# Edge convolutions of a graph network: maxima stored and edge attributes loaded in six pieces a turn

## The chip, the cores and the metric

The kernel runs on one core of one Trainium2 chip. The metric is the device time of one execution in microseconds (us), the median of several runs. TensorE (PE) does matrix products, VectorE (DVE) and ScalarE (ACT) work on vectors, GpSimd (POOL) here issues gathers by index, and SyncE (SP) issues plain transfers. All transfers share the core's 16 DMA engines.

## What is computed

A four-part graph network on 3125 nodes of 96 features and 50,000 edges, sorted by destination: 16 propagation steps, two layers of neighbour sums, a weighted neighbour sum, and at the end two edge convolutions, with a layer norm after each part. The change touches the edge convolutions alone:

```python
def _egnn_conv(x, src, dst, edge_attr, W_msg, W_edge, W_root, b):
    msg = x[src] @ W_msg + edge_attr @ W_edge
    agg = jax.ops.segment_max(msg, dst, num_segments=x.shape[0])
    agg = jnp.where(jnp.isneginf(agg), 0.0, agg)
    return agg + x @ W_root + b
c1 = jax.nn.leaky_relu(_egnn_conv(X, src, dst, edge_attr, W1_msg, W1_edge, W1_root, b1))
c2 = jax.nn.leaky_relu(_egnn_conv(c1, src, dst, edge_attr, W2_msg, W2_edge, W2_root, b2))
```

## The kernel before

The edges stand as 128 streams (one a partition) of T = 392 edges each. `edge_conv` runs once a layer. It goes over the 392 steps in TN = 14 turns of TURN = 28 tiles; a tile is 128 edges, one of each stream. Tiles 0 to 9 of a turn (PICKS = 10) get their source rows from PE: ten one-hot matrices times the table `yparts`, in 25 blocks of nodes (`pick`), and the edge term is added by `close`. Tiles 10 to 27 get theirs by 18 gathers that POOL issues from the table `y_table` in DRAM; their edge terms are made by PE in four groups of 5, 5, 5 and 3 tiles (`EGROUPS`, `edge_terms`), and DVE adds them (`add_terms`). DVE then runs the running maximum along the stream, tile by tile (`ran` counts the tiles). The one-hots of a turn are made by DVE (17 blocks) and ACT (8 blocks). At a turn's end ACT copies the picked rows out of PSUM (`take_rows`).

The work overlaps across turns: in turn k PE makes the edge terms of turn k and the picks of turn k + 1, POOL gathers for turn k + 1, each gather only after so many pick blocks are done (`used`), and DVE runs the maxima of turn k. The messages `msg` and the edge attributes `ea` have two buffers each, by the parity of the turn.

Three streams of transfers belong to a turn, all issued by SP in a fixed order:
- `store_run`: the running maxima go to DRAM (`run_max`), in two stores (`STORES`): tiles 0 to 19 (960 KB) when `ran` says that tile 20 is done, and tiles 20 to 27 (384 KB) at the turn's end.
- `load_ea`: the edge attributes of turn k + 2 come in one load of 896 KB, issued between the two stores, once PE has made the last edge terms of turn k (`terms`).

POOL and DVE write the buffer of turn k again in turn k + 2, after the semaphores `rst` of the stores; PE waits for `eal` of the load before `close` and `edge_terms`. At the layer's start SP issues both first loads and then the store of the node table to `y_table`, which POOL's first gather waits for (`yst`). At the layer's end POOL waits for all stores of `run_max` and then gathers 25 times from it (the last edge of each node), and the result is put together.

## Time and profile before

| | us |
|---|---|
| median of 3 runs | 2619.41 |
| lowest and highest | 2613.77, 2621.47 |
| the profiled execution | 2614.05 |
| its span | 2612.3 |
| edge convolution, layer 0 (1587.11 to 2096.30) | 509.2 |
| edge convolution, layer 1 (2096.30 to the end) | 516.0 |
| one turn (ACT's first copy to its first copy in the next turn) | 27.8 to 31.0 |
| mean granted clock of PE | 0.897 of full |

The profile is of one execution. Its time is the span and 1.75 us around it. Times of rows are us from the span's start. A row of the timeline gives start, duration, engine, line, operation, what it writes and reads, the number of merged instructions, and in brackets the engine's idle time before it and what ended that; "remote" stands for a semaphore whose sender the profile doesn't match, "issue" for idle time with no wait that it shows. "SPq" is a transfer's issue by SP. The ends of matmuls are modelled.

### The profile page before, as it was taken

The page shows a single profiled execution, that of the slowest core. Times are in us where ns is not written, and L with a number is a line of the kernel's source. Part 1 is how long each engine was busy: PE and PEld are TensorE (multiplying, and loading weights), DVE is VectorE, ACT ScalarE, POOL GpSimd, SP SyncE. Part 2 cuts the span into 40 slices and gives each one's busy share as a digit, 9 for nine tenths or more (in the row PEclk, how much of TensorE's full clock was granted, in tenths as well). Part 3 has the DMA queues.
Part 4 walks back from the last instruction along what each step waited for, and adds up shares of the span by engine and source line. Part 5 has one row for each costly group of instructions (what it writes and reads, how often), then busy time and mean ns, then how long its engine had stood idle before and what let it go on. Part 6 is the DMA issues. An engine that isn't in the chain of part 4 may idle for free. (4 is left out here: it accounts for less than half of the span.)

```text
span 2612.3 us, 54694 instructions
## 1 busy us (share of the span) xinstructions
PE 2108.3 (81%) x21375; PEld 1855.4 (71%) x21375; DVE 1616.7 (62%) x4651; ACT 879.5 (34%) x1209; POOL 1181.3 (45%) x997
## 2 busy tenths in 40 slices
PE   4494579999999999997876977888886578888860
PEld 4232279999999999997872436777776577777760
DVE  7999975555555555574572034766665356676656
ACT  0495510000000000001210005887784067788720
POOL 0200057887878777720000003666564346566641
PEclk9995579999999999998987986999998589999975
DMA  3592012323233223310007822344333034334321
GB/s 127 179 408 107 1 23 20 30 21 30 21 30 26 24 20 30 30 17 7 2 1 313 318 94 69 115 130 130 111 111 111 19 96 131 113 110 128 121 77 28
DMA packets 150904, 227.14 MB, mean 87 GB/s; under 512 B 87649, under 2 KB 109825, under 8 KB 147106
## 3 DMA queue, kind: packets, MB, share of 16 engines
q1 hardware_dynamic: 70994, 186.72, 19.6%
q0 software_dynamic: 74688, 28.51, 11.4%
q10 hardware_dynamic: 5008, 9.07, 1.1%
q8 instruction: 134, 2.20, 0.3%
q14 instruction: 80, 0.66, 0.1%
HBM read 123.37 MB, written 100.84 MB: 86 GB/s over the span
## 5 line engine op out<-in xcount | busy, mean ns | idle before, releaser
L615 PE MATMUL ps<-parts,at 128*128 128x192 f16 x11250 | 948.1, 248 | 23.4 <-POOL at L647 13.4
L615 PEld LDWEIGHTS ps<-parts,at 128*128 128x128 f16 x11250 | 940.3, 99 | 25.6 <-issue 24.0
L1622 PE MATMUL ps<-yparts,source_onehots_c 128*128 128x192 f16 x7000 | 675.5, 253 | 129.8 <-issue 110.0
L1413 POOL DMA_INDIRECT messages_c<-y_table,srci_sb x504 | 495.6, 983 | 571.9 <-DMA y_table<-ytab 259.4
L1622 PEld LDWEIGHTS ps<-yparts,source_onehots_c 128*128 128x128 f16 x7000 | 590.0, 101 | 199.6 <-issue 156.8
L656 POOL DMA_INDIRECT weight_matrix<-w,place x392 | 608.7, 1553 | 162.2 <-issue 95.6
L1441 ACT ACTIVATE source_gaps_c<-sources_spread,unshift 128x1280 f16<-128x1280 f16 x216 | 294.8, 1365 | 19.3 <-PE ps L1622 3.2
L739 DVE SCALAR_TENSOR_TENSOR t<-ps,coef,g 128x96 f32<-128x96 f32 x400 | 127.0, 317 | 250.3 <-PE ps L615 211.6
L1444 ACT ACTIVATE source_onehots_c<-source_gaps_c 128x1280 f16<-128x1280 f16 x216 | 274.4, 1270 | 6.9
L684 ACT ACTIVATE ea_limbs<-ea_in,ea_scale 128x392 f16<-128x392 f32 x32 | 19.9, 621 | 744.0 <-DMA ea_in<-in_eaT 738.8
L1496 DVE TENSOR_SCALAR source_onehots_c<-sources_spread,shift 128x1280 f16<-128x1280 f16 x484 | 264.9, 557 | 0.3
L1545 DVE SCALAR_TENSOR_TENSOR messages_c<-messages_c,brk 128x96 f32<-128x96 f32 x784 | 249.3, 318 | 18.2
L605 PE MATMUL ps<-onekey,oneplace 128*128 128x200 f16 x784 | 154.9, 359 | 80.5 <-DVE oneplace L560 80.5
L605 PEld LDWEIGHTS ps<-onekey,oneplace 128*128 128x128 f16 x784 | 78.9, 122 | 156.4 <-DVE oneplace L560 108.1
L1516 DVE TENSOR_TENSOR messages_c<-picked_pairs_c 128x192 f32<-128x192 f32 x140 | 49.2, 351 | 175.2 <-issue 132.3
L1244 PE MATMUL ps<-weights,x_sb 128*96 128x512 f32 (+1 forms) x350 | 137.1, 555 | 24.0 <-DMA weights<-weight_matrix 24.0
L742 DVE SCALAR_TENSOR_TENSOR t<-ps,coef,t 128x96 f32<-128x96 f32 x400 | 127.2, 318 | 14.1
L1524 DVE TENSOR_TENSOR messages_c<-messages_c,ps 128x480 f32<-128x480 f32 x112 | 67.1, 599 | 108.1 <-remote 102.6
L1244 PEld LDWEIGHTS ps<-weights,x_sb 128*96 128x96 f32 x350 | 55.2, 165 | 106.1 <-issue 81.8
L749 DVE CAST parts<-t 128x96 f16<-128x96 f32 x375 | 92.4, 246 | 55.6 <-DVE t L742 1.0
L1453 ACT ACTIVATE picked_pairs_c<-ps 128x384 f32<-128x384 f32 x140 | 57.7, 498 | 192.7 <-remote 153.5
L647 POOL TENSOR_TENSOR at<-at,ident 128x128 f16<-128x128 f16 x25 | 10.8, 470 | 244.5 <-issue 244.5
(359 smaller groups left out, 1540.2 us busy)
## 6 DMA issues: line engine op xcount, KB each, us to landing
weight_matrix<-blank SPq DMA_DIRECT2D x27, 1600.0 KB
weights<-weight_matrix SPq DMA_DIRECT2D x27, 1600.0 KB, 9.6
run_max<-messages_c SPq DMA_DIRECT2D x28, 960.0 KB
ea_c<-edge_limbs SPq DMA_DIRECT2D x28, 896.0 KB
edge_limbs<-ea_limbs SPq DMA_DIRECT2D x128, 98.0 KB
run_max<-messages_c SPq DMA_DIRECT2D x28, 384.0 KB
sources_spread<-sources_by_tile ACTq DMA_DIRECT2D x26, 320.0 KB
messages_c<-y_table,srci_sb POOLq DMA_INDIRECT x504
```

The source lines that it names most:

```text
L605: nc.tensor.matmul(m.ps[:, n % 8, 256 * (s % 2):256 * (s % 2) + KEYS], oneplace[:, q % RING, h, :, j], onekey[:, q % RING, h, :, j], start ...
L615: mm = nc.tensor.matmul(m.ps[:, bank, 0:2 * D], m.at[:, s, blk * P:(blk + 1) * P], parts[:, s, :], start=(s == 0), stop=(s == NB - 1))
L656: nc.gpsimd.indirect_dma_start(cells, bass.IndirectOffsetOnAxis(m.place[:, t:t + 1], 0), m.w[:, t:t + 1], None, compute_op=ALU.add).then_i ...
L739: nc.vector.scalar_tensor_tensor(t1[:, r % 2, :], m.ps[:, r % NBK, 0:D], coef[:, i:i + 1], g0[:, i, :], ALU.mult, ALU.add).then_inc(tmp1, 1)
L742: nc.vector.scalar_tensor_tensor(t2[:, r % 2, :], m.ps[:, r % NBK, D:2 * D], coef[:, i:i + 1], t1[:, r % 2, :], ALU.mult, ALU.add).then_in ...
L1244: mm = nc.tensor.matmul(m.ps[0:D, a // CW, 0:n], rows, mt[:, k % R, a:a + n], start=(k == 0), stop=(k == MB - 1))
L1413: nc.gpsimd.indirect_dma_start(msg[:, k % 2, j, :], None, d.yt, bass.IndirectOffsetOnAxis(m.srci[:, k * TURN + j:k * TURN + j + 1], 0)).th ...
L1441: nc.scalar.activation(gap[:], srcb[:, k % 2, :, :].rearrange("p i e -> p (i e)"), ACT.Abs, bias=m.unshift[:, b:b + 1]).then_inc(gapd, 1)
L1444: nc.scalar.activation(hot[:, b, :], gap[:], ACT.Relu, bias=1.0, scale=-1.0).then_inc(hota, 1)
L1496: nc.vector.tensor_scalar(hot[:, b, :], srcb[:, k % 2, :, :].rearrange("p i e -> p (i e)"), m.shift[:, b:b + 1], None, ALU.is_equal).then_ ...
L1545: nc.vector.scalar_tensor_tensor(msg[:, k % 2, j, :], prev, m.brk[:, TURN * k + j:TURN * k + j + 1], msg[:, k % 2, j, :], ALU.add, ALU.max ...
L1622: mm = nc.tensor.matmul(m.ps[:, i // 2, at:at + 2 * D], hot[:, b, i * P:(i + 1) * P], parts[:, b, :], start=(b == 0 and i % 2 == 0), stop= ...
```

## The change

Stores and loads of a turn go in the same six pieces of 5, 5, 5, 5, 5 and 3 tiles (`PIECES`). A piece of the maxima is stored (240 KB, the last 144 KB) once `ran` says that its last tile is done. The edge attributes of turn k + 2 are loaded piece by piece (160 KB, the last 96 KB): pieces 0, 1 and 2 right behind the store of piece 2, and pieces 3, 4 and 5 each behind the store of the same number, after waits on `terms` that grow by one edge group a piece. The two semaphores `rst` of a side now count four pieces (tiles 0 to 19) and two pieces (tiles 20 to 27); `eal` counts six loads. The waits of POOL, DVE and PE stand where they stood, with the new counts. At a layer's start twelve loads stand ahead of the store to `y_table`, where there were two. Bytes, and all instructions of PE, DVE, ACT and POOL, are the same.

```diff
-STORES = ((0, EGROUPS[2][0]), (EGROUPS[2][0], TURN - EGROUPS[2][0]))
+PIECES = ((0, 5), (5, 5), (10, 5), (15, 5), (20, 5), (25, 3))
+HALF = 4
...
-            load_ea(0)
-            load_ea(1)
+            for k in range(2):
+                for a, n in PIECES:
+                    load_ea(k, a, n)
             sp.dma_start(d.yt.rearrange("(i p) f -> p i f", p=P), m.ytab[:]).then_inc(yst, 16)
             for k in range(TN):
-                sp.wait_ge(ran, TURN * k + STORES[1][0] + 1)
-                store_run(k, 0)
-                if k + 2 < TN:
-                    sp.wait_ge(terms, NEG * k + NEG)
-                    load_ea(k + 2)
-                sp.wait_ge(ran, TURN * k + TURN)
-                store_run(k, 1)
+                for x, (a, n) in enumerate(PIECES):
+                    sp.wait_ge(ran, TURN * k + a + n)
+                    store_run(k, x // HALF, a, n)
+                    if k + 2 < TN and x >= 2:
+                        sp.wait_ge(terms, NEG * k + x - 1)
+                        if x == 2:
+                            for first in (0, 1):
+                                load_ea(k + 2, *PIECES[first])
+                        load_ea(k + 2, a, n)
...
                         if k >= 2 and j == PICKS:
-                            g.wait_ge(rst[k % 2][0], 16 * (k // 2))
-                        if k >= 2 and j == STORES[1][0]:
-                            g.wait_ge(rst[k % 2][1], 16 * (k // 2))
+                            g.wait_ge(rst[k % 2][0], 16 * stores[0] * (k // 2))
+                        if k >= 2 and j == PIECES[HALF][0]:
+                            g.wait_ge(rst[k % 2][1], 16 * stores[1] * (k // 2))
...
-                pe.wait_ge(eal[odd], 16 * half + 16)
+                pe.wait_ge(eal[odd], 16 * len(PIECES) * half + 16 * len(PIECES))
```

SP's queue of the kernel before, two turns in the middle of a layer; a row is a transfer, with the shape of one:

```order
66 L1374 DMA run_max<-messages_c 128x1920
67 L1370 DMA ea_c<-edge_limbs 128x3584
68 L1374 DMA run_max<-messages_c 128x768
69 L1374 DMA run_max<-messages_c 128x1920
70 L1370 DMA ea_c<-edge_limbs 128x3584
71 L1374 DMA run_max<-messages_c 128x768
```

SP's queue of the changed kernel, from the end of the layer's start over the first turn; rows that read alike are merged (x3):

```order
61 L1372 DMA ea_c<-edge_limbs 128x384
62 L1380 DMA y_table<-ytab 128x25x96
63 L1375 DMA run_max<-messages_c 128x480 x3
64 L1372 DMA ea_c<-edge_limbs 128x640 x3
65 L1375 DMA run_max<-messages_c 128x480
66 L1372 DMA ea_c<-edge_limbs 128x640
67 L1375 DMA run_max<-messages_c 128x480
68 L1372 DMA ea_c<-edge_limbs 128x640
69 L1375 DMA run_max<-messages_c 128x288
70 L1372 DMA ea_c<-edge_limbs 128x384
```

Three transfers a turn have become twelve: the first three stores stand ahead of the first loads, and the rest alternate, a store and a load. The last store of a turn has 288 values a partition, where it had 768.

## Rows read from the trace of the kernel before

**Rows 1.** Page, part 1: busy us, share of the span, instructions.

```profile
PE 2108.3 (81%) x21375; PEld 1855.4 (71%) x21375; DVE 1616.7 (62%) x4651; ACT 879.5 (34%) x1209; POOL 1181.3 (45%) x997
```

**Rows 2.** Windows: us; busy (x) of PE, PEld, DVE, ACT, POOL; PEclk, DMA share, GB/s.

```profile
2134.76:2163.40 28.64, 23.78 (x278) 21.50 (x278) 19.42 (x54) 23.00 (x22) 17.75 (x18) 1.00 0.41 124
2163.40:2191.20 27.80, 23.66 (x278) 21.48 (x278) 19.52 (x54) 22.93 (x21) 17.78 (x18) 1.00 0.40 125
...
2279.70:2308.30 28.60, 24.18 (x278) 21.38 (x278) 19.43 (x54) 22.96 (x21) 18.15 (x19) 1.00 0.39 121
2308.30:2338.00 29.70, 24.96 (x278) 22.43 (x278) 19.56 (x54) 23.07 (x21) 17.86 (x18) 0.94 0.37 120
```

**Rows 3.** Timeline: PE's last edge terms, and who starts when their semaphore arrives.

```profile
2298.58 0.29 PE L1645 MATMUL ps<-w_limbs_c,ea_c 128*128 128x96 f16 x3
...
2302.15 0.33 SPq L1370 DMA_DIRECT2D ea_c<-edge_limbs  x1
2302.16 0.45 DVE L1524 TENSOR_TENSOR messages_c<-messages_c,ps 128x288 f32<-128x288 f32 x1 [3.68 <-remote]
```

**Rows 4.** Windows: stretches of one turn, few and many transfers; columns of rows 2.

```profile
2140.76:2150.76 10.00, 9.37 (x117) 8.96 (x115) 9.72 (x27) 9.35 (x8) 6.63 (x7) 1.00 0.29 66
2150.76:2154.76 4.00, 3.87 (x50) 3.70 (x48) 2.69 (x8) 3.90 (x4) 2.67 (x4) 1.00 0.74 274
```

**Rows 5.** Waits (us in total, times, longest) of SP and DVE, 2131 to 2510.

```profile
SPq L1374 <- DVE messages_c L1545: 326.3, 21, 53.7
SPq L1370 <- remote: 68.6, 12, 6.1
...
DVE messages_c L1524 <- remote: 52.1, 18, 4.2
```

**Rows 6.** Timeline: SP's issues at the start of layer 1, first gather, first uses.

```profile
2096.30 0.81 SPq L1370 DMA_DIRECT2D ea_c<-edge_limbs  x2
2097.16 0.43 SPq L1378 DMA_DIRECT2D y_table<-ytab  x1
...
2108.68 1.01 POOL L1413 DMA_INDIRECT messages_c<-y_table,srci_sb  x1 [54.86 <-DMA y_table<-ytab]
...
2134.76 2.02 ACT L1453 ACTIVATE picked_pairs_c<-ps 128x384 f32<-128x384 f32 x5 [16.47 <-PE ps L1631]
...
2143.03 0.64 DVE L1524 TENSOR_TENSOR messages_c<-messages_c,ps 128x480 f32<-128x480 f32 x1
```

**Rows 7.** Timeline, layer 1: PE during and after POOL's first run of gathers.

```profile
2115.80 0.49 PE L1622 MATMUL ps<-yparts,source_onehots_c 128*128 128x192 f16 x4 [0.48 <-issue]
...
2125.33 0.95 POOL L1413 DMA_INDIRECT messages_c<-y_table,srci_sb  x1 [0.30 <-issue]
...
2128.56 4.65 PE L1622 MATMUL ps<-yparts,source_onehots_c 128*128 128x192 f16 x32 [0.39 <-issue]
```

**Rows 8.** Timeline, layer 0: the same, from the first gather on.

```profile
1599.73 1.47 POOL L1413 DMA_INDIRECT messages_c<-y_table,srci_sb  x1 [204.52 <-DMA y_table<-ytab]
...
1610.40 0.50 PE L1622 MATMUL ps<-yparts,source_onehots_c 128*128 128x192 f16 x4 [0.47 <-issue]
...
1620.88 0.95 POOL L1413 DMA_INDIRECT messages_c<-y_table,srci_sb  x1 [0.30 <-issue]
...
1624.64 0.60 PE L1645 MATMUL ps<-w_limbs_c,ea_c 128*128 128x96 f16 x5
```

**Rows 9.** Timeline, layer 1's end: SP's last two stores, last maxima, first gather.

```profile
2523.98 3.16 SPq L1374 DMA_DIRECT2D run_max<-messages_c  x2
...
2525.77 1.03 DVE L1545 SCALAR_TENSOR_TENSOR messages_c<-messages_c,brk 128x96 f32<-128x96 f32 x3
...
2529.88 0.94 POOL L1420 DMA_INDIRECT source_onehots_c<-run_max,endi  x1 [18.09 <-DMA run_max<-messages_c]
```

**Rows 10.** Windows: the transfers of two stretches; columns of rows 2.

```profile
2304.00:2306.00 2.00, 1.84 (x27) 1.43 (x25) 0.01 (x1) 0.00 (x0) 1.14 (x2) 1.00 0.95 394
2097.00:2103.00 6.00, 6.00 (x46) 5.74 (x47) 6.00 (x14) 5.87 (x5) 0.00 (x0) 0.61 0.95 310
```

More of the change, by code:

```diff
@@ L1346, in edge_conv @@
         rst = [[sem(f"run_{side}_{h}_stored") for h in range(2)] for side in "ab"]
+        stores = (HALF, len(PIECES) - HALF)
         lt, sc, ct, cc = sem("last_turned"), sem("carries"), sem("carry_turned"), sem("carry_copied")
@@ L1367, in _, with load_ea, store_run @@
             limbs = d.eas.rearrange("l q t e -> (l q) t e")
-            def load_ea(k):
-                sp.dma_start(ea[:, k % 2, :, :], limbs[:, k * TURN:(k + 1) * TURN, :]).then_inc(eal[k % 2], 16)
-            def store_run(k, h):
-                a, n = STORES[h]
+            def load_ea(k, a, n):
+                sp.dma_start(ea[:, k % 2, a:a + n, :], limbs[:, k * TURN + a:k * TURN + a + n, :]).then_inc(eal[k % 2], 16)
+            def store_run(k, h, a, n):
                 sp.dma_start(rdram[:, k * TURN + a:k * TURN + a + n, :], msg[:, k % 2, a:a + n, :]).then_inc(rst[k % 2][h], 16)
-            load_ea(0)
-            load_ea(1)
+            for k in range(2):
+                for a, n in PIECES:
+                    load_ea(k, a, n)
             sp.dma_start(d.yt.rearrange("(i p) f -> p i f", p=P), m.ytab[:]).then_inc(yst, 16)
             for k in range(TN):
-                sp.wait_ge(ran, TURN * k + STORES[1][0] + 1)
-                store_run(k, 0)
-                if k + 2 < TN:
-                    sp.wait_ge(terms, NEG * k + NEG)
-                    load_ea(k + 2)
-                sp.wait_ge(ran, TURN * k + TURN)
-                store_run(k, 1)
-            for r in rst[0] + rst[1]:
-                sp.wait_ge(r, 16 * (TN // 2))
+                for x, (a, n) in enumerate(PIECES):
[7 more added lines that the diff above has]
+                        load_ea(k + 2, a, n)
+            for side in rst:
+                for h in range(2):
+                    sp.wait_ge(side[h], 16 * stores[h] * (TN // 2))
             sp.wait_ge(yst, 16)
@@ L1415, in _ @@
                                                                                0)).then_inc(got[k % 2][e], 16)
-            for r in rst[0] + rst[1]:
-                g.wait_ge(r, 16 * (TN // 2))
+            for side in rst:
+                for h in range(2):
+                    g.wait_ge(side[h], 16 * stores[h] * (TN // 2))
             for i in range(NB):
@@ L1531, in _ @@
                 if k >= 2:
-                    v.wait_ge(rst[k % 2][0], 16 * (k // 2))
+                    v.wait_ge(rst[k % 2][0], 16 * stores[0] * (k // 2))
                 for j in range(TURN):
@@ L1638, in edge_terms @@
                 a, n = EGROUPS[e]
-                pe.wait_ge(eal[odd], 16 * half + 16)
+                pe.wait_ge(eal[odd], 16 * len(PIECES) * half + 16 * len(PIECES))
                 if e >= EBANKS:
```

## The prediction, made before the changed kernel ran

> **What bounds the kernel now.** I read the page's busy shares first, then windows of single turns, then the timeline of one turn, SP's waits, and last the two ends of a layer. PE is the busiest engine, 81% of the span, and DVE has 62% [rows 1]; an average over stages, so the turns were read by themselves. In a turn of layer 1 PE is busy 23.7 to 25.0 of 27.8 to 29.7 us, ACT about 23, DVE 19.5, POOL 18, and the transfers take 0.37 to 0.41 of the 16 DMA engines [rows 2]. So no transfer can be the bound by its volume. PE holds the turn: the copies of ACT that end a turn wait for it, and the next picks of PE wait for these copies.
>
> The next question is what PE, DVE and POOL wait for inside a turn, and whether a store or a load is ever the last to come. DVE waits before its last add of a turn, 3.68 us by "remote" [rows 3], 52.1 us over 13 turns [rows 5]. That add waits for two things, PE's last edge terms and three gathers. Which one is late shows in SP: its load of edge attributes waits for the edge terms alone, and its issue starts at 2302.15, DVE's add at 2302.16 [rows 3]. Both were released by the same semaphore, so it was PE's, although its matmuls are recorded 3.3 us earlier (their ends are modelled). The gathers had landed. SP itself stands waiting for DVE's maxima 326.3 us (some 33 of them before the stretch, in its first wait of 53.7) and for the edge terms 68.6 us, together 362 of 379 us [rows 5]. It is idle nearly all the time and nobody waits for it inside a turn.
>
> The buffers are far from tight as well. The load for turn k + 2 is issued near the end of turn k, and `close` needs it at the end of turn k + 1, some 28 us later. The stores of turn k must be out before DVE and POOL write that buffer for turn k + 2. POOL comes first there: its gathers for turn k + 2 begin with the first picks of turn k + 1. The first store's data move from about 2150.76 to 2154.76 [rows 4], 8.6 us before its turn ends at 2163.40 [rows 2] and those gathers begin; the second half's first tile is gathered more than 10 us after that. Nothing the change makes earlier is waited for.
>
> **The change part by part.** The sum is made against the profiled execution, 2614.05 us (span 2612.3 and 1.75 around it). The median of the three runs is 2619.41, 5.4 us above it, so I give the result on the median's scale: median plus the change's sum.
>
> *Middle of a layer.* Nine more issues a turn on SP. Two issues take 0.81 us [rows 6], so about 0.4 each, 3.6 us a turn; SP waits 362 of 379 us [rows 5], so this is hidden. The cover ends only if SP's work came near 28 us a turn; it will be 12 x 0.4 = 4.9. The waits on `terms` are free: piece x is stored after the maximum of its last tile, which needs the add of edge terms that the wait asks for or a later one. So the old wait of up to 6.1 us [rows 5] for the last edge terms goes away, and it is worth nothing, since only the store of 384 KB stood behind it and that waits for a later maximum anyway. The loads get earlier, which is worth nothing either (28 us of slack).
>
> What could still move is the work beside the transfers. Today the large transfers lie in the last 12 us of a turn. Ten microseconds of the first turn with a DMA share of 0.29 hold 117 matmuls (11.7 a us), the next four with a share of 0.74 hold 50 (12.5 a us) [rows 4]. PE is not slower beside them, so moving them into the earlier part costs nothing, and taking them out of the later part gives nothing. Bounds from whole turns: the first turn of layer 1 has no store or load in its first 16 us and lasts 28.64, the second 27.80, a later one at the same full clock 28.60 [rows 2]. Of transfers I would say between 0 and 0.8 us a turn; I take 0, because the turn with the fewest transfers is the longest of the three. Both ends go into the range: 0 to -0.8 x 24 = -19 us, and half of that the other way, +10 us, since six of the twelve pieces (stores and loads 0 to 2) move to a part of the turn that has no transfers now.
>
> *Layer's start.* Twelve loads are issued where two were, so the store to `y_table` is issued 10 x 0.4 = 4.1 us later, at about 2101.3 in place of 2097.16 [rows 6]. Its data stand behind the same 1792 KB of loads either way; at the 394 GB/s of a stretch with two transfers queued [rows 10] these take 4.7 us from about 2097.3, until 2102. The issue at 2101.3 and about 1 us to the first packet gives 2102.3. So the first gather comes 0.3 us later, with bounds of 0 and 4.1 (if the small loads don't overlap). What waits for the gathers: DVE's first add at 2143.03, 34 us after the first gather at 2108.68 [rows 6]; hidden. But PE goes slowly while POOL gathers without a pause: in layer 1 it is down to 4 matmuls and a pause from 2115.80 on and is at full pace again from 2128.56, 2.3 us after the last gather of that run [rows 7]; in layer 0 from 1610.40 to 1624.64, 2.8 us after the last of 18 gathers [rows 8]. If the end of that slow stretch hangs on the gathers, a later first gather moves the first turn by its full delay: +0.3 us a layer, up to +4.1. I take +0.3 x 2 = +0.6.
>
> *Layer's end.* The last maximum ends at 2526.80 and the first gather from `run_max` starts at 2529.88, 3.08 us later [rows 9], for the last store of 384 KB. That is 1.0 us of data at 394 GB/s [rows 10]; the last piece has 144 KB, 0.37 us. The rest, 2.1 us, is issue and completion and stays. Saved: 0.6 us a layer, -1.2 us in all; bounds 0 and -1.0 a layer, the whole time of the data. The same 3.1 us stand in layer 0.
>
> Here a rule of the Trainium skill speaks against the change: "DMA: Bandwidth & Descriptors", section Bandwidth, says to batch transfers to 1 MiB or more for three quarters of the peak, and the same page (Anatomy of one DMA) fits 2.0 us fixed and 436 GB/s to a transfer. An estimate from it: 2.0 + 0.34 = 2.3 us for the last piece against 2.0 + 0.90 = 2.9 us now, a saving of 0.6 us, the same as from the rows; and twelve transfers of 160 to 240 KB, were they to run one behind the other, 29 us a turn in place of 11. By that the queue would be as long as the turn. The trace has three transfers one behind the other at 310 GB/s over 6 us, starting pause included [rows 10], so their fixed parts overlap, and I don't charge it.
>
> *Sum:* 0 + 0.6 - 1.2 = -0.6 us, on the profiled execution 2613.4, on the median 2618.8. I say 2619 us: no change.
>
> **The rivals.**
> *Faster, transfers in the way (a).* Large rows of the stores hold the gathers and PE back at each turn's end; pieces free them. Price 0.8 us in each of 24 turns, 19 us, at 2600. For it: DVE's wait by "remote" lies right behind the first store. Against it: 2302.15 beside 2302.16, and PE's pace in rows 4. The skill has the mechanism (same page, Queues, rings and completion order: an engine takes turns between queues a whole packet at a time); no row shows a late gather being waited for. Chance 0.14.
> *Faster, layer's start (b).* If the gathers start later, PE has more of its first picks done before it gets slow. In layer 0 it had 31 matmuls left at 1610.40, 2.3 us of work. A delay of 2.5 us or more would let it finish first, some 11 us earlier, at 2608 with layer 0 alone. It decides from a delay of 2.5 us; I expect 0.3. Chance 0.08.
> *Slower, the queue's start (c).* The small loads don't overlap as I think, the first gather comes 4.1 us later in both layers, PE's slow stretch ends 4.1 us later with it, and the turns with transfers spread over them lose a quarter us each: +8 +6 = +14, at 2633. It decides from a delay of some 4 us. Against it: 310 GB/s over the present start. Chance 0.12.
> *Slower, the queue as the bound (d).* Each piece takes the 3.1 us of the last store alone: twelve make 37 us, 9 more than a turn, +200 us. Spoken against by the share of 0.95 at 394 GB/s with two transfers queued [rows 10]. Chance 0.02.
> *Clock.* A turn at a granted clock of 0.94 takes 29.70 us, one at 1.00 28.60 [rows 2]. Shifts of a few tenths of a us can move a turn from one kind to the other; four turns more or fewer are 4 us, inside the main case.
>
> **How the numbers follow.** A measurement of this kernel can tell about 0.3%, 7.9 us, from no change. Main case: 2619 within 5 us of clock and ends, chance 0.64. Faster by more than 0.3%: most of (a) and (b), 0.21. Slower: (c) and (d), 0.12, of which a part of (c) stays within 0.3%. That gives 0.21, 0.67 and 0.12. The range takes the main case, (a) and half of (c): 2599 to 2629.
>
> **What would show it.** Right: a turn at full clock between 27.8 and 28.7 us as before; DVE's last add still waits some 3.7 us; first gather within 0.5 us of 12.4 us behind the layer's start; from last maximum to first gather of `run_max` 2.5 us. Wrong by (a): turns 0.5 us or more shorter at the same clock, DVE's wait gone. By (b) or (c): the time from a layer's start to ACT's first copy, 38.5 us now, changes by more than 1 us.

## The result

Before: median 2619.72 us (2613.77 to 2625.49, 20 runs). Changed: median 2625.3 us (2620.85 to 2632.72, 20 runs). The ratio is 1.0022, 95% interval 1.0015 to 1.0030. The changed kernel is 5.6 us slower. That is inside the range that was given and under the 0.3% that I had taken as the least that can be told. But the interval of this comparison doesn't contain 1, so the loss is real, and its sign is the other one: the sum had -0.6 us.

The profiled executions differ by more than the medians: spans of 2612.3 and 2624.2 us, 11.9 apart. The execution of before lay 5.7 us under its median, the one of the changed kernel (2625.94) 0.6 over its own. So a term read from the two traces is good to some microseconds when it is a sum over turns, and much better when it is one interval between two instructions that wait for each other.

Read from the two traces, us; a layer starts with DVE's first memset:

| | before, layers 0 and 1 | changed, layers 0 and 1 |
|---|---|---|
| layer's start to first gather | 12.5, 12.3 | 14.8, 14.0 |
| layer's start to ACT's first copy | 38.3, 38.4 | 41.0, 39.9 |
| 13 turns (first copy of turn 0 to that of turn 13) | 380.3, 378.0 | 383.9, 381.4 |
| last maximum to first gather of `run_max` | 3.09, 3.08 | 2.52, 2.50 |
| from there to the next layer, or the end | 73.5, 82.4 | 75.4, 83.0 |

The last line is work that the change doesn't touch. In the traces of the experiments on chips of the same kind (see below) it lies between 70.9 and 76.4 us for layer 0 and between 82.4 and 83.2 for layer 1, so its +1.9 and +0.6 are taken as the scatter of single executions.

The lines of the changed kernel are shifted: L1372 is the load (L1370), L1375 the store of maxima (L1374), L1380 the store to `y_table` (L1378), L1418 the gather (L1413), L1426 the gather from `run_max` (L1420), L1459 ACT's copy (L1453), L1522 the add of a pair of picks (L1516), L1530 the add of edge terms (L1524), L1551 the maximum (L1545), L1628 the pick (L1622), L1637 `close` (L1631), L1651 the edge terms (L1645).

The page of the changed kernel, part 1, the line of part 3 for SP's queue, and PE's pick in part 5. It answers to [rows 1].

```profile
PE 2110.1 (80%) x21375; PEld 1859.3 (71%) x21375; DVE 1616.8 (62%) x4651; ACT 879.7 (34%) x1209; POOL 1184.1 (45%) x997
q1 hardware_dynamic: 107282, 186.73, 20.4%
L1628 PE MATMUL ps<-yparts,source_onehots_c 128*128 128x192 f16 x7000 | 676.2, 254 | 126.8 <-issue 99.0
```

The work is the same to the instruction and to 2 us of PE's time. The same line of part 3 before has 70994 packets and 19.6%: the same bytes in one and a half times as many packets, for 0.8 points more of the engines' time.

Windows of the changed kernel, columns as in [rows 2]: five turns of layer 1, then the 13 turns of each layer.

```profile
2143.34:2172.98 29.64, 25.13 (x278) 23.00 (x278) 19.95 (x54) 22.96 (x22) 17.62 (x18) 0.91 0.43 120
2172.98:2201.64 28.66, 24.18 (x278) 21.50 (x278) 19.73 (x54) 22.96 (x21) 17.77 (x18) 1.00 0.44 124
...
2261.45:2289.46 28.01, 23.93 (x278) 21.47 (x278) 19.75 (x54) 22.96 (x21) 17.63 (x18) 1.00 0.43 124
2289.46:2319.92 30.46, 25.35 (x278) 22.68 (x278) 19.70 (x54) 23.18 (x21) 17.61 (x19) 0.94 0.41 117
2319.92:2348.78 28.86, 24.19 (x278) 21.46 (x278) 19.63 (x54) 22.96 (x21) 18.02 (x18) 1.00 0.42 122
```
```profile
1627.70:2011.56 383.86, 327.17 (x3624) 294.12 (x3624) 253.23 (x693) 288.41 (x266) 232.39 (x234) 0.94 0.40 116
2143.34:2524.71 381.37, 324.44 (x3624) 291.07 (x3624) 253.23 (x693) 288.74 (x265) 230.20 (x234) 0.95 0.41 116
```

And the 13 turns of each layer in the kernel before:

```profile
1625.38:2005.71 380.33, 323.27 (x3623) 290.84 (x3624) 252.82 (x693) 288.54 (x265) 229.87 (x235) 0.96 0.38 117
2134.76:2512.77 378.01, 321.15 (x3624) 287.63 (x3624) 251.95 (x693) 288.50 (x265) 230.52 (x234) 0.97 0.38 117
```

Turns whose granted clock is 1.00 take 28.0 to 28.9 us here and 27.9 to 28.9 before, but for the eleventh turn of a layer, which takes some 31 us at that clock (both layers before, layer 0 changed). What is longer is the sum, by 3.5 and 3.4 us a layer, with the mean granted clock down by 0.02 and PE's busy time up by 3.9 and 3.3. Read turn by turn, 10 of the 26 turns before have a granted clock of 1.00, and 6 of 26 in the changed kernel. With the 1.1 us between a turn at 1.00 and one at 0.94 in [rows 2], an estimate, four such turns are 4.4 of the 6.9 us. The share of the transfers rose from 0.38 to 0.40 or 0.41 for the same bytes.

The timeline of the changed kernel at the two starts, SP and the first gather, then PE and ACT of layer 1. It answers to [rows 6, 7, 8].

```profile
1586.57 6.99 SPq L1372 DMA_DIRECT2D ea_c<-edge_limbs  x12
1593.60 0.43 SPq L1380 DMA_DIRECT2D y_table<-ytab  x1
...
2103.34 6.40 SPq L1372 DMA_DIRECT2D ea_c<-edge_limbs  x12
...
2109.78 0.43 SPq L1380 DMA_DIRECT2D y_table<-ytab  x1
2117.38 1.43 POOL L1418 DMA_INDIRECT messages_c<-y_table,srci_sb  x1 [58.33 <-DMA y_table<-ytab]
...
2126.10 0.49 PE L1628 MATMUL ps<-yparts,source_onehots_c 128*128 128x192 f16 x4 [0.67 <-issue]
...
2143.34 2.02 ACT L1459 ACTIVATE picked_pairs_c<-ps 128x384 f32<-128x384 f32 x5 [18.01 <-remote]
```

The twelve loads take SP 7.0 and 6.4 us, 0.58 and 0.53 each in the mean. The store to `y_table` is issued 7.0 and 6.4 us behind the layer's start; before it was 0.9. The mean hides how this comes about. The twelve issues of each layer, with the shortest, median and longest in ns:

```profile
L1372 SPq DMA_DIRECT2D ea_c<-edge_limbs x12: 333/432/1869, 1586.6 to 1593.1; - x12
L1372 SPq DMA_DIRECT2D ea_c<-edge_limbs x12: 333/432/1081, 2103.3 to 2109.3; - x12
```

Most of them take 0.43 us, as the second of the two loads did before (0.33 and 0.43), and stand 0.47 us apart from start to start. On top comes one long issue, the fourth in both layers, of 1.87 and 1.08 us (in layer 1 another of 0.63).

The waits of the changed kernel from 2138 to 2525, and the end of layer 1 in its timeline. They answer to [rows 5] and [rows 9].

```profile
SPq L1375 <- DVE messages_c L1551: 257.0, 53, 37.9
SPq L1372 <- remote: 0.4, 2, 0.2
...
DVE messages_c L1530 <- remote: 54.2, 21, 4.2
```
```profile
2537.68 1.03 DVE L1551 SCALAR_TENSOR_TENSOR messages_c<-messages_c,brk 128x96 f32<-128x96 f32 x3
...
2541.21 0.95 POOL L1426 DMA_INDIRECT source_onehots_c<-run_max,endi  x1 [17.51 <-DMA run_max<-messages_c]
```

SP's wait for the edge terms is gone (68.6 to 0.4 us), and SP still stands idle for 257 of 387 us. DVE's waits before its adds of edge terms have stayed (52.1 and 54.2). From the last maximum to the gather it is now 2.50 us.

### The profile page after: what moved, and what is told of

The parts are those of the page before. It is cut to its first block and busy times, and to the rows that moved or that the text cites. A ratio compares the mean times of both kernels' runs of the same rounds, so it can differ in the third digit from the quotient of the medians.

```text
span 2624.2 us, 54946 instructions
## 1 busy us (share of the span) xinstructions
PE 2110.1 (80%) x21375; PEld 1859.3 (71%) x21375; DVE 1616.8 (62%) x4651; ACT 879.7 (34%) x1209; POOL 1184.1 (45%) x997
## 5 line engine op out<-in xcount | busy, mean ns | idle before, releaser
L616 PE MATMUL ps<-parts,at 128*128 128x192 f16 x11250 | 947.1, 247 | 24.7 <-POOL at L648 14.8
L1628 PE MATMUL ps<-yparts,source_onehots_c 128*128 128x192 f16 x7000 | 676.2, 254 | 126.8 <-issue 99.0
L1418 POOL DMA_INDIRECT messages_c<-y_table,srci_sb x504 | 497.9, 988 | 582.2 <-DMA y_table<-ytab 264.7
L1628 PEld LDWEIGHTS ps<-yparts,source_onehots_c 128*128 128x128 f16 x7000 | 593.6, 101 | 196.1 <-issue 150.0
L1551 DVE SCALAR_TENSOR_TENSOR messages_c<-messages_c,brk 128x96 f32<-128x96 f32 x784 | 249.5, 318 | 18.2
L1522 DVE TENSOR_TENSOR messages_c<-picked_pairs_c 128x192 f32<-128x192 f32 x140 | 49.2, 352 | 177.7 <-issue 111.3
L1530 DVE TENSOR_TENSOR messages_c<-messages_c,ps 128x480 f32<-128x480 f32 x112 | 67.3, 601 | 115.3 <-remote 107.5
L1459 ACT ACTIVATE picked_pairs_c<-ps 128x384 f32<-128x384 f32 x140 | 57.8, 498 | 203.7 <-remote 199.6
```

Of the source, the lines that this page charges most:

```text
L616: mm = nc.tensor.matmul(m.ps[:, bank, 0:2 * D], m.at[:, s, blk * P:(blk + 1) * P], parts[:, s, :], start=(s == 0), stop=(s == NB - 1))
L1418: nc.gpsimd.indirect_dma_start(msg[:, k % 2, j, :], None, d.yt, bass.IndirectOffsetOnAxis(m.srci[:, k * TURN + j:k * TURN + j + 1], 0)).th ...
L1551: nc.vector.scalar_tensor_tensor(msg[:, k % 2, j, :], prev, m.brk[:, TURN * k + j:TURN * k + j + 1], msg[:, k % 2, j, :], ALU.add, ALU.max ...
L1628: mm = nc.tensor.matmul(m.ps[:, i // 2, at:at + 2 * D], hot[:, b, i * P:(i + 1) * P], parts[:, b, :], start=(b == 0 and i % 2 == 0), stop= ...
```

## Experiments

Three questions: is the start what costs, does the end give what was worked out, and do pieces inside the turns cost anything. Kernels of one group below ran on one chip, and each ratio is against the kernel before on that chip, with its 95% interval. Chips differ, so times of different groups aren't compared. A cost in microseconds is the ratio's distance from 1 times the median of before; the difference of the two medians can be 2 us off it.

### First group: the parts alone (before 2630.19 us, 35 runs)

**The changed kernel with two whole loads at the start.**

```diff
             for k in range(2):
-                for a, n in PIECES:
-                    load_ea(k, a, n)
+                load_ea(k, 0, TURN)
...
-                pe.wait_ge(eal[odd], 16 * len(PIECES) * half + 16 * len(PIECES))
+                pe.wait_ge(eal[odd], 16 * len(PIECES) * half + 16)
```

> The changed kernel with its two first loads whole again, as before the change; all pieces inside the turns stay. Theory A (the loss is made at the layers' starts: twelve issues of 0.58 us put the first gather 2.3 and 1.7 us later, and ACT's first copy follows the first gather by 26 us): first gather back at +12.4 us from the layer's start, first copy at +38.3, and the time at the kernel before's -1.2 to +1, ratio 0.9995 to 1.0005. Rival B (the pieces inside the turns cost, 3.5 us a layer in the one profiled execution): first copy at +38.3 too, but the time stays 4 to 6 us above the kernel before, ratio 1.0015 to 1.0025.

Measured: 2633.38 us, ratio 1.0012 (1.0003 to 1.0021), +3.2 us. The start is back: first gather 12.3 and 11.8 us behind the layer's start, first copy 38.0 and 38.2. The end is the short one, 2.51 us, which gives back 1.2. The ratio lies between the two forecasts. By the medians something else costs 4.4 us (3.2 + 1.2; 2.0 to 6.7 by the interval), and only the pieces inside the turns are left. The traces of this group don't show it: the 13 turns take 776.9 us over both layers here, and between 773.5 and 776.9 in the three kernels below, whose turns are as before (one has pieces in the last turn). So this cost stands on one interval alone.

**The kernel before with twelve loads at the start.**

```diff
-            load_ea(0)
-            load_ea(1)
+            for k in range(2):
+                for a, n in PIECES:
+                    sp.dma_start(ea[:, k % 2, a:a + n, :],
+                                 limbs[:, k * TURN + a:k * TURN + a + n, :]).then_inc(eal[k % 2], 16)
```

> The kernel before with twelve first loads in pieces in place of two; turns as before. Theory A: first gather at +14 to +15 us from the layer's start, first copy 1.5 to 2.8 us later than before in each layer, and the time 3 to 5.5 us above the kernel before, ratio 1.0012 to 1.002. Rival B: the same delay of the first gather, but under 1 us in the time, ratio 0.9995 to 1.0005.

Measured: 2633.73 us, ratio 1.0020 (1.0011 to 1.0029), +5.3 us. The timeline at the start of layer 0:

```profile
1585.08 6.26 SPq L1379 DMA_DIRECT2D ea_c<-edge_limbs  x12
1591.38 0.43 SPq L1380 DMA_DIRECT2D y_table<-ytab  x1
1599.47 1.55 POOL L1415 DMA_INDIRECT messages_c<-y_table,srci_sb  x1 [205.91 <-DMA y_table<-ytab]
```

First gather 14.3 and 14.6 us behind the layer's start, 2.0 and 2.7 more than in the run above; first copy 39.3 and 40.0, 1.2 and 1.7 more. That is 3.0 us by the trace and 2.9 to 7.6 by the interval. The start alone is enough to make this kernel slower. A single pair of traces is a coarse measure here: the kernel with pieces in the last turn alone (below), whose start is that of before, has its first gather at 13.7 and 12.7 us and its first copy at 39.3 and 37.8.

**The kernel before with the store to `y_table` ahead of the two loads.**

```diff
+            sp.dma_start(d.yt.rearrange("(i p) f -> p i f", p=P), m.ytab[:]).then_inc(yst, 16)
             load_ea(0)
             load_ea(1)
-            sp.dma_start(d.yt.rearrange("(i p) f -> p i f", p=P), m.ytab[:]).then_inc(yst, 16)
```

> The kernel before with the store of the node table issued ahead of the two first loads: a layer's first gather comes earlier by the data of the loads, about 4.7 us. If PE's slow stretch hangs on the gathers (first copy = first gather + 26 us), the first copy comes about 4.7 us earlier and the time falls by 9 us, ratio 0.9965. If the first copy has a bound of its own at +38.3 us, the time stays within 1 us, ratio 0.9997 to 1.0003. If PE is caught by its slow stretch with more picks left to do, it could also be slower by a few us.

Measured: 2626.33 us, ratio 0.9989 (0.9980 to 0.9999), -2.9 us. Its timeline at the start of layer 0:

```profile
1585.27 0.37 SPq L1376 DMA_DIRECT2D y_table<-ytab  x1
1585.69 5.39 SPq L1370 DMA_DIRECT2D ea_c<-edge_limbs  x2
1593.24 2.74 POOL L1413 DMA_INDIRECT messages_c<-y_table,srci_sb  x1 [199.72 <-DMA y_table<-ytab]
```

First gather 7.9 and 7.6 us behind the layer's start, first copy 36.1 and 35.3: 1.9 and 2.9 us less than with the two whole loads first. From issue to gather the store takes 8.0 us with nothing ahead of it, and 7.9 and 7.6 in the changed kernel, where the loads were issued over the 7.0 and 6.4 us ahead of it. The forecast was a first copy 4.7 us earlier and a ratio of 0.9965; half of the shift arrives, and a third of the gain. In the kernel before the store took 11.5 to 11.8 from issue to gather, because it was issued at once and its data stood behind the loads. So in the changed kernel the data of the loads hide behind their own issues, and what is left is the issues. The timeline above also shows that an issue has no fixed price: the two loads took 0.81 us with nothing ahead of them [rows 6], and take 5.39 and 5.20 us behind the store.

**The kernel before with stores in pieces in the last turn alone.**

```diff
-            for k in range(TN):
+            for k in range(TN - 1):
...
+            k = TN - 1
+            for x, (a, n) in enumerate(PIECES):
+                sp.wait_ge(ran, TURN * k + a + n)
+                sp.dma_start(rdram[:, k * TURN + a:k * TURN + a + n, :],
+                             msg[:, k % 2, a:a + n, :]).then_inc(rst[k % 2][x // HALF], 16)
```

> The kernel before with the stores in six pieces in a layer's last turn alone. From the last maximum to the first gather of the stored maxima 2.5 us in place of 3.1, so 0.6 us a layer; the time 1.2 us below the kernel before, ratio 0.9995, near the limit of what can be told. If it is at or above 1.0, the end of a layer isn't bound by that gather.

Measured: 2630.39 us, ratio 1.0002 (0.9993 to 1.0011). Last maximum to first gather 2.51 us in both layers, 0.58 less each. The trace shows the gain and the time can't: 1.2 us are 0.05% and the interval is 0.18% wide.

### Second group: stores, loads, more pieces, the gathers (before 2615.23 us, 23 runs)

**Stores in six pieces, loads whole.**

```diff
+                for x, (a, n) in enumerate(PIECES):
+                    sp.wait_ge(ran, TURN * k + a + n)
+                    store_run(k, x // HALF, a, n)
+                    if k + 2 < TN and x == 4:
+                        sp.wait_ge(terms, NEG * k + NEG)
+                        load_ea(k + 2, 0, TURN)
```

> Stores in six pieces in every turn; the load of a turn is whole, behind the store of piece 4; the first loads whole. Theory S (the stores make the cost in the turns, as three of them move into a part of the turn that had no transfers): ratio to the kernel before 1.001, as with all pieces in the turns (1.0012 measured). Theory L (the loads make it): ratio 0.9995 to 1.0002, the saving at the layer's end alone.

Measured: 2613.15 us, ratio 0.9994 (0.9982 to 1.0005); 13 turns 379.4 and 376.6 us, last maximum to gather 2.52.

**Loads in six pieces, stores as before** (whole loads at the start).

```diff
+                for x, (a, n) in enumerate(PIECES):
+                    sp.wait_ge(ran, TURN * k + (a + n if x != 3 else STORES[1][0] + 1))
+                    if x == 3:
+                        store_run(k, 0)
+                    if x == 5:
+                        store_run(k, 1)
+                    if k + 2 < TN and x >= 2:
+                        sp.wait_ge(terms, NEG * k + x - 1)
...
+                        load_ea(k + 2, a, n)
```

> Loads of a turn in six pieces at the places of the changed kernel, the two stores as before, the first loads whole. Theory L: ratio to the kernel before 1.001 to 1.0015. Theory S: 0.9997 to 1.0005.

Measured: 2616.47 us, ratio 1.0004 (0.9994 to 1.0015); 13 turns 380.5 and 378.7 us. Neither kind alone shows a cost. By the ratios, and with the stores' shorter end taken out (1.2 us), they cost -0.4 and +1.0 us, together some +0.7 with 4 us either way. The first run of the first group has 4.4 for both (2.0 to 6.7), so the two don't contradict each other, and neither names the kind.

**Both in fourteen pieces of two tiles** (whole loads at the start), to make a cost of the pieces large.

```diff
-PIECES = ((0, 5), (5, 5), (10, 5), (15, 5), (20, 5), (25, 3))
-HALF = 4
+PIECES = tuple((a, 2) for a in range(0, TURN, 2))
+HALF = 10
+FIRST = 7
```

> Stores and loads of every turn in fourteen pieces of two tiles (96 and 64 KB) in place of six, the first loads whole. If the cost in the turns (about 3 to 4 us with six pieces) grows with the number of transfers, 28 in place of 12 a turn where 3 stood: cost 25/9 of it, 8 to 11 us, ratio 1.003 to 1.004. If it comes from where in the turn the bytes move, not from their number, ratio 1.001 to 1.0015 as with six. If the measured 1.0012 was chance, 0.9995 to 1.0005.

Measured: 2633.52 us, ratio 1.0068 (1.0049 to 1.0086), +17.8 us. Its windows of 13 turns, and its waits of SP from 2131 to 2520:

```profile
1624.16:2017.15 392.99, 337.40 (x3624) 300.58 (x3624) 254.45 (x693) 290.28 (x265) 231.03 (x235) 0.91 0.42 113
2143.29:2532.50 389.21, 332.38 (x3629) 296.55 (x3626) 252.51 (x693) 290.07 (x266) 234.10 (x234) 0.93 0.42 114
```
```profile
SPq L1376 <- DVE messages_c L1551: 165.5, 81, 39.0
```

With 28 transfers a turn, pieces cost, twice what had been forecast from their number (1.003 to 1.004). The turns take 782.2 us over both layers, against 756.0 with stores in six pieces and 759.2 with loads in six on this chip. The kernel with the late gathers (below) has the turns of before; without the first turn of a layer, it takes 701.5 us, and the three kernels with pieces 725.3 (fourteen), 698.2 (stores in six) and 701.1 (loads in six). So fourteen pieces cost 24 us by the traces, and six of one kind nothing that a trace shows. SP isn't why: it still waits 165.5 us for maxima. PE's time has grown: it is busy 669.8 us, against 643.0 with the stores in six pieces, at a granted clock of 0.91 and 0.93 against 0.96 and 0.97. More of its matmuls fall under the lower of the clock's two levels. I can't say from this which came first, a PE that is held up more often, or the clock.

**The kernel before, POOL's first gather held back until PE has done all 25 blocks of its first picks.**

```diff
+            g.wait_ge(used, NB)
```

> The kernel before, but POOL starts its first gather of a layer only when all 25 blocks of the first picks are done. If PE's slow stretch at the layer's start comes from the gathers, PE goes through the first picks without it: first copy at +24 to +28 us from the layer's start in place of +38.3, and up to 20 us less in all, unless the gathers, 13 us later, then hold up DVE's first adds or slow PE in the next turn: the gain kept is between 0 and 20 us, ratio 0.992 to 1.0. If the slow stretch comes from PE's own instructions (the same position in its program, whatever POOL does), the first copy stays at +38 us or later and the time is the same or higher.

Measured: 2631.76 us, ratio 1.0066 (1.0049 to 1.0083). Its timeline in layer 0:

```profile
1586.25 23.28 PE L1623 MATMUL ps<-yparts,source_onehots_c 128*128 128x192 f16 x250 [3.29 <-DVE source_onehots_c L1497]
...
1609.72 2.02 ACT L1454 ACTIVATE picked_pairs_c<-ps 128x384 f32<-128x384 f32 x5 [2.13 <-PE ps L1632]
...
1610.32 0.94 POOL L1414 DMA_INDIRECT messages_c<-y_table,srci_sb  x1 [216.60 <-PE ps L1623]
...
1620.27 0.34 PE L1623 MATMUL ps<-yparts,source_onehots_c 128*128 128x192 f16 x1 [0.40 <-issue]
1621.69 0.32 PE L1623 MATMUL ps<-yparts,source_onehots_c 128*128 128x192 f16 x1 [1.07 <-issue]
1622.40 0.32 PE L1623 MATMUL ps<-yparts,source_onehots_c 128*128 128x192 f16 x1 [0.39 <-issue]
...
1642.79 5.53 PE L1623 MATMUL ps<-yparts,source_onehots_c 128*128 128x192 f16 x46 [0.37 <-issue]
1642.99 0.66 DVE L1525 TENSOR_TENSOR messages_c<-messages_c,ps 128x480 f32<-128x480 f32 x1 [21.20 <-remote]
```

This is the run that shows what the start of a layer hangs on. Held back by 12 us, the gathers leave PE alone and the first copy comes at 24.1 us, 14 earlier. But then they run without a pause beside the next turn's picks, PE goes down to one or two matmuls per 0.7 to 1.4 us (at most 2.8) from 1616.69 to 1642.79, and the first turn takes some 53 us. The expectation had a gain of 0 to 20 us; the loss is 17 us. The slow stretch moves with the gathers. It begins 6 us behind the first of them and ends 3.4 us after the last of the run. So the start of a layer is a place where a stall is passed on, and a gather that comes later is paid for in one turn or in the next.

### Third and fourth group: stores against loads, and a better start

**Stores alone in fourteen pieces, and loads alone in fourteen pieces.** The stores' loop of the run of fourteen with `load_ea(k + 2, 0, TURN)` behind the thirteenth store, and its loads' loop with the two old stores. In the stores' kernel:

```diff
+                    if k + 2 < TN and x == 12:
+                        sp.wait_ge(terms, NEG * k + NEG)
+                        load_ea(k + 2, 0, TURN)
```

In the loads' kernel:

```diff
+                    if x == 10:
+                        store_run(k, 0)
+                    if x == 13:
+                        store_run(k, 1)
+                    if k + 2 < TN and x >= FIRST:
```

> Stores alone in fourteen pieces of two tiles in every turn; the load of a turn whole behind the store of piece 12, the first loads whole. With both in fourteen pieces the ratio to the kernel before was 1.0068. If the loads are what costs (they went 1.0004 alone in six pieces, the stores 0.9994): ratio 0.999 to 1.001. If the number of transfers costs, whichever they are: about half of 0.0068, 1.003 to 1.004.

> Loads alone in fourteen pieces of two tiles in every turn, the two stores as before (the first one maximum later), the first loads whole. If the loads are what costs: ratio to the kernel before 1.005 to 1.008. If the number of transfers costs, whichever they are: 1.003 to 1.004. If the cost comes only of both together (they alternate in SP's queue): 1.0 to 1.001.

Measured: before 2406.68 us (35 runs); stores 2403.6, ratio 0.9991 (0.9982 to 1.0000); loads 2406.78, ratio 1.0003 (0.9992 to 1.0013). The kernel before itself takes 209 to 224 us less here than on the chips of the first two groups, so something that slows it there is missing, and this chip may not be the place to ask. The repeats below say what is missing.

**Stores in six pieces with the `y_table` store first; and the `y_table` store first with pieces in the last turn alone,** on the same chip as the two above.

```diff
+            sp.dma_start(d.yt.rearrange("(i p) f -> p i f", p=P), m.ytab[:]).then_inc(yst, 16)
             load_ea(0)
             load_ea(1)
...
+            k = TN - 1
+            for x, (a, n) in enumerate(PIECES):
```

> Stores in six pieces, the load of a turn whole, the first loads whole, and the store of the node table ahead of them. The sum of what was measured alone: 0.9994 for the stores and 0.9989 for the table first, so 0.9983, 4 to 5 us below the kernel before. First gather at +7.7 us from the layer's start, first copy at +35 to +36.5.

> The kernel before with the store of the node table first and with stores in six pieces in the last turn of a layer alone. Table first alone went 0.9989, the last turn alone 1.0002 (0.5 us a layer by the trace): 0.9985, 3 to 5 us below the kernel before. If it is as fast as the kernel with stores in pieces in all turns, what these stores bring lies at the layer's end alone.

Measured: 2403.8 us, ratio 0.9996 (0.9987 to 1.0005), and 2403.97, ratio 0.9988 (0.9978 to 0.9999). The first misses its forecast of 0.9983, a sum of gains from chips of the other kind. In the second the first gather comes 8.0 and 6.7 us behind the layer's start and the first copy 24.0 and 23.3; in the first it is 7.3 and 6.6, and 23.9 and 23.3.

**The changed kernel again, and three of the above again** (before 2404.08 us, 33 runs), with no edit.

> The changed kernel once more, beside the parts of it on one chip. If PE has its slow stretches on this chip (first copy at +38 us, turns of 29 to 30 us): ratio to the kernel before 1.002 as first measured, first copy 1.5 to 2.8 us later. If PE has none (first copy at +24, turns of 23.8 us, as in the runs on the last chip): the later first gather is hidden, the layer's end saves 1.2 us, ratio 0.999 to 1.0005.

> Stores alone in fourteen pieces again; on the last chip, where PE had no slow stretch, 0.9991. Where PE has slow stretches: if the number of transfers costs, 1.003 to 1.004; if the loads are what costs, 0.999 to 1.001. Without slow stretches 0.9991 again.

> Loads alone in fourteen pieces again; on the last chip, where PE had no slow stretch, 1.0003. Where PE has slow stretches: if the loads are what costs, 1.005 to 1.008; if the number of transfers costs, 1.003 to 1.004; if only both together, 1.0 to 1.001. Without slow stretches 1.0003 again.

> Table first and the last turn's stores in pieces again; 0.9988 on the last chip. Where PE has slow stretches: table first alone went 0.9989 with the first copy 2 to 3 us earlier in each layer, and the layer's end gives 0.6 us: 0.9983 to 0.9989. If the gain of table first comes through PE's slow stretch alone, it is 0.9995 where there is none.

Measured: the changed kernel 2404.79 us, ratio 1.0005 (0.9996 to 1.0014); stores in fourteen 2404.07, 1.0000 (0.9991 to 1.0009); loads in fourteen 2403.29, 0.9993 (0.9984 to 1.0002); table first and last turn 2403.6, 0.9994 (0.9984 to 1.0004). This chip is of the same kind as the third group's. Two lines of the changed kernel's page here, of parts 1 and 5, its windows (13 turns of layer 1, its first turn), and its timeline at the start of layer 1:

```profile
PE 2034.5 (85%) x21375; PEld 1828.8 (76%) x21375; DVE 1621.0 (68%) x4651; ACT 878.2 (37%) x1209; POOL 1197.4 (50%) x997
L1628 PE MATMUL ps<-yparts,source_onehots_c 128*128 128x192 f16 x7000 | 615.9, 247 | 36.0 <-ACT picked_pairs_c L1459 25.3
```
```profile
2009.04:2318.60 309.56, 294.75 (x3619) 281.33 (x3617) 254.70 (x693) 287.94 (x266) 237.95 (x236) 1.00 0.50 143
2009.04:2032.85 23.81, 23.10 (x289) 21.96 (x286) 19.78 (x54) 22.87 (x21) 18.33 (x19) 1.00 0.51 148
```
```profile
1985.72 5.57 SPq L1372 DMA_DIRECT2D ea_c<-edge_limbs  x12
...
1991.33 0.43 SPq L1380 DMA_DIRECT2D y_table<-ytab  x1
1999.02 1.24 POOL L1418 DMA_INDIRECT messages_c<-y_table,srci_sb  x1 [30.79 <-DMA y_table<-ytab]
...
2009.04 2.02 ACT L1459 ACTIVATE picked_pairs_c<-ps 128x384 f32<-128x384 f32 x5 [1.33 <-PE ps L1637]
```

The idle time ahead of PE's picks by "issue" is no longer what stands in the line: 126.8 us of idle time have become 36.0, and what is left is mostly ACT's. A turn takes 23.8 us in place of 28 to 31, at the full clock. The twelve loads take SP 5.57 us, with no long issue among them, and the first gather still comes 13.9 and 13.2 us behind a layer's start. But ACT's first copy stands at 23.8 and 23.2, where it ends its wait for PE; with two whole loads (stores in fourteen pieces) it is 24.2 and 23.8. Nobody waits for the gathers, so the changed start costs nothing.

**Stores and loads in fourteen pieces once more** (before 2403.67 us, 21 runs).

> The kernel before with the stores of the maxima in fourteen pieces of two tiles and the loads of the attributes whole, sent again for a chip whose PE has slow stretches beside POOL's gathers (turns of 29 us). Theory A, the stores' pieces are what lengthens the turns (they share their way with POOL's gathers): ratio 1.004 to 1.008 and a mean turn 0.4 to 0.9 us above that of before. Theory B, the loads' pieces do: 0.999 to 1.001, of which the shorter end of both layers gives back 1.3 us. Theory C, only the count of pieces matters: 1.002 to 1.004. Where PE has no slow stretches (turns of 24 us), all three give 0.999 to 1.001.

> The kernel before with the loads of the attributes in fourteen pieces of two tiles from the third on (the first two whole) and the stores as they were, for the same chip. Theory A (the stores' pieces): 0.999 to 1.001. Theory B (the loads' pieces): 1.004 to 1.008, with a mean turn 0.4 to 0.9 us above that of before. Theory C (the count of pieces): 1.002 to 1.004. Where PE has no slow stretches, all three give 0.999 to 1.001.

Measured: 2403.65 us, ratio 0.9998 (0.9989 to 1.0007), and 2403.87, ratio 0.9999 (0.9990 to 1.0008). The chip was again one without slow stretches, where all three theories expect the same. In three comparisons, on two chips, neither kind cost anything there, with 14 transfers a turn in place of one or two. Which kind costs beside slow stretches stays open.

## Why the prediction was wrong

**Layer's start: the term that failed, by its size.** The prediction had +0.6 us for both layers; the traces have +2.8 and +1.5, the experiment with the start alone 2.9 to 7.6. The failed step is the price of an issue of SP, "about 0.4 each" [rows 6], read from two issues of 0.81 us: 5.0 us for twelve, where they take 7.0 and 6.4. The store to `y_table` is issued 6.1 and 5.5 us later, and not 4.1. Of what is missing, 2.0 and 1.4 us, some 0.7 us is the distance from start to start, 0.47 where I had 0.41, and the rest are the long issues (1.4 and 0.8 us above the usual 0.43). So it isn't that each of twelve costs more: the twelfth took 0.43 us, as the second did before. It is that among many issues one is held up, and two issues with nothing ahead of them couldn't show that; why the fourth is held up no run tells. Of the first gather's place, 14.8 and 14.0 us behind the start where I had 12.7, the later issue explains nearly all: 2.0 and 1.4 of 2.1 and 1.3. The place itself follows the prediction's own sum with the right number in it: the store's data go about 1 us after its issue, so at 8.0 and 7.4 us in place of 5.7, which is 2.3 and 1.7 later, as measured.

**What the delay does was right.** "A later first gather moves the first turn by its full delay." Before, ACT's first copy comes 25.8 and 26.1 us behind the first gather; in the changed kernel 26.2 and 26.0. Within the first group about six tenths of a shift arrive: of 2.0 and 2.7 us with twelve loads 1.2 and 1.7, of 4.5 and 4.2 the other way with the table first 1.9 and 2.9. Over all traces from this kind of chip nearly all of it does: six with two whole loads at the start (late gathers and table first left out) have the first gather at 12.8 and 12.2 us in the mean and the first copy at 38.4 and 38.1, the two with twelve loads 14.6 and 14.3, and 40.1 and 39.9. The late gathers show the link itself, since the slow stretch moves with them.

**Rival (c)** had this mechanism, at 4.1 us a layer, and it is the one that came nearest: a delay of 2.3 and 1.7 us, and turns a little longer. Its price was +14, the measured time +5.6. **Rival (b)** needed 2.5 us of delay to let PE finish its first picks; 2.3 us in layer 0 didn't do it, nor did 2.7 in layer 1 of the kernel with twelve loads alone. That the effect exists the late gathers show (first copy 14 us earlier), and also that it is no gain, since the slow stretch falls into the next turn. **(a)** is out: no turn at the full clock got half a microsecond shorter, and DVE's waits before the adds of edge terms are there as before (54.2 us in all, the longest 4.2). **(d)** is out: SP idles 257 us.

**Layer's end: right.** 3.09 to 2.52 and 3.08 to 2.50 us, -0.6 each, as the rows had it. The fit of the Trainium skill ("DMA: Bandwidth & Descriptors", Anatomy of one DMA) gives the same saving. The page states it for transfers that GpSimd issues; for these, issued by SP, its estimates of 2.9 and 2.3 us are 0.2 below the measured ones.

**Middle of a layer: by the medians not 0, and inside its bounds.** I let the turns stand, within -19 and +10 us. The traces say +6.9, of two executions of which one lay 5.7 us under its median and the other at it; the changed kernel without its start says 4.4 (2.0 to 6.7), by its medians and not by its trace. The argument from [rows 4], that PE isn't slower beside a transfer, compared stretches with the same few large transfers. It said nothing of more, smaller ones. Both in fourteen pieces cost 17.8 us. The same page of the Trainium skill, section Bandwidth, asks for batches of 1 MiB or more, and this rule, which I had not charged, has the right sign here. It is a rule on bandwidth, and bandwidth isn't what the traces show as the limit: the share of the DMA engines went up by 0.02 to 0.04 only, to 0.42 at most over 13 turns, and it is PE whose busy time grows.

The terms: start +4.3, end -1.2, middle from the first group +4.4, together +7.5 with some 2.4 us of uncertainty in the last; measured +5.6 to the medians. Nothing large is missing, though no run has all three on one chip. What failed is thus one duration, which alone turns the sign (+4.3 against -1.2), and a middle set to zero, which the medians put at some 4 us. How six pieces a turn cost these 4 us, and whether by the stores or the loads, stays open. The prediction allowed the clock 4 us either way, and the trace of the changed kernel has four fewer turns at full clock; no trace with six pieces tells whether the pieces or chance bring them.

## What to carry to other kernels

Before splitting a transfer, count what stands behind it in the same queue: a chain that starts with a store pays for every issue ahead of it, here 0.47 us each, plus 0.7 to 1.4 us a layer for those that were held up. Putting that store first was the only edit with ratios whose whole interval lies below 1 (0.9989 alone; 0.9988 with the last turn in pieces, which came to 0.9994, not distinguishable from 1, when it was repeated). Split only the transfer that somebody waits for, the last of a layer here, and not the 26 for which nobody does. A price read from two issues with nothing ahead of them is the usual price; it says nothing of an issue that is held up, and in a row of twelve there was one.

## What the runs showed of the hardware

The kernel before takes 2615 to 2630 us in the main comparison and the first two groups, and 2404 to 2407 us in the later three, 8% less. The difference lies in the edge convolutions: the changed kernel's layer 0 starts at 1586.7 us on one kind of chip and at 1586.1 on the other. There it lies in PE beside POOL's gathers. On the first kind PE drops, some 6 to 11 us into an unbroken run of gathers, to a group of one to four matmuls per 0.7 to 1.4 us and recovers 2 to 4 us after the last gather of the run; on the other kind it doesn't, and a turn takes 23.8 us in place of 29.2. The stretch from the first gather of `run_max` to the end of a layer, with its 25 gathers, is shorter as well (49.0 and 65.0 us in the changed kernel, 75.4 and 83.0 on the first kind). The idle time ahead of PE's picks that the profile puts down to "issue" is 99.0 us in the changed kernel on the first kind; on the second all idle time ahead of them is 36.0. Why the chips differ no run here tells. It does tell that a verdict on this kernel holds for a kind of chip: the change costs 0.22% on one and nothing that can be measured (1.0005) on the other.
